# A state-space stage rewritten: convolutions on TensorE, the scan in two halves of the tokens with its input in PSUM

## The chip, the cores and the metric

One core of a Trainium2 chip runs the whole program. The metric is the device time of one execution in microseconds, the median of three runs. The engines are TensorE (PE; its weight loads are PEld), VectorE (DVE), ScalarE (ACT), GpSimd (POOL) and SyncE (SP, which here only issues transfers).

## The reference, cut to what matters

The program is a small transformer of eight sublayers on x of shape (1, 2048, 128), each followed by a residual add and a layer norm. The change touches the fifth sublayer, a selective state-space layer:

```python
def _L2_attn_ref(x, W_in, conv_x_w, conv_x_b, conv_z_w, conv_z_b, W_xdbl, W_dt, inv_dt, D, W_out, b_out):
    xz = x @ W_in
    xs, z = jnp.split(xz, 2, axis=-1)
    A = -jnp.tile(jnp.arange(1, D_STATE + 1, dtype=jnp.float32), (D_HALF, 1))
    xs = jax.nn.silu(_dw_conv(xs, conv_x_w, conv_x_b))   # 4 taps along the tokens, per channel
    z = jax.nn.silu(_dw_conv(z, conv_z_w, conv_z_b))
    x_dbl = xs @ W_xdbl
    dt_low, Bc, Cc = jnp.split(x_dbl, [DT_RANK, DT_RANK + D_STATE], axis=-1)
    dt = dt_low @ W_dt + inv_dt
    delta = jax.nn.softplus(dt + inv_dt)
    y = _selective_scan(xs, delta, A, Bc, Cc, D)
    y = jnp.concatenate([y, z], axis=-1)
    return y @ W_out + b_out
# _selective_scan, for each of 16 states n and each of 128 channels, over 2048 tokens:
#   h = exp(delta * A[n]) * h + (delta * u) * B[n];  y += h * C[n];  at the end y += u * D
```

## The kernel before

Everything stays in SBUF in float32. Activations lie as 128 channels (partitions) by 2048 tokens; PSUM has eight banks of 512 columns, so work goes in blocks of 512 tokens, numbered 0 to 3. Each stage is a class with one method for each engine (`pe`, `act`, `dve`, `pool`) that writes the engine's instructions in a fixed order by hand; engines meet only at counters (`wait_ge`, `then_inc`) and at a barrier (`Barrier.meet`, L128) where a stage begins. The state-space stage is `Mamba` (L1284).

**Entry.** PE turns x into its transpose XT before the barrier. Then it projects blocks of xs (L1348) and z (L1358); ACT copies them to SBUF with a margin of zeros (L1462, L1470). DVE does the convolution of xs as four shifted multiply-adds for each block (`taps`, L1594 and L1597), ACT applies silu to give U (L1468). PE multiplies U by W_xdbl (L1365, 64 rows for delta; L1368, 32 rows for B and C). B and C are split into three bfloat16 parts by turns between ACT and DVE (L1479 to L1488, L1544, L1549) and stored in SPL. PE makes dt (L1379), ACT its absolute value, exponential and logarithm (L1492, L1494, L1498), DVE the rest of the softplus and delta*u, called DU (L1554, L1559, L1561), for all 2048 tokens before the scan begins.

**Loop over the 16 states.** A selecting matmul of bfloat16 spreads row n of B over the 128 partitions, a block at a time (`rows_b`, L1441, PSUM banks 0 and 1). DVE multiplies that by DU into the SBUF tile H (`scale_in`, L1604). ACT makes the decay DA = exp(-(n+1)*delta) for 2048 tokens (L1517). DVE runs one scan over 2048 tokens (L1571) in place:

```python
            e.tensor_tensor_scan(h, da, h, 0.0, ALU.mult, ALU.add).then_inc(self.scan.sem)
```

`rows_c` (L1450, banks 2 and 3) spreads row n of C, ACT copies it to SBUF (`copy_c`, L1524, four buffers CS), POOL multiplies H by it in place (L1618), and PE adds the 16 products up in banks 4 to 7 with float32 matmuls by the identity (`add_up`, L1454). H has three buffers, DA two. The four taps of the convolution of z run on DVE over all 2048 tokens after states 1, 5, 9 and 13 (L1594, L1597).

**Tail.** ACT applies silu to z (L1508), DVE adds u*D (L1583), PE multiplies by W_out (L1416, L1417), DVE and ACT do the layer norm (L300 to L335).

## Time and profile before

| | |
|---|---|
| median of 3 runs | 2852.85 us (2852.33 to 2854.08) |
| the profiled execution | 2858.49 us, its span 2856.7 us |
| busy share of the span | PE 87%, DVE 73%, ACT 50%, POOL 43% |
| mean granted TensorE clock | 0.937 of full speed |
| the state-space stage, from its barrier to the next one | 685.3 to 905.3 us of the span |

A row names a line of the kernel, an engine, an operation and its tiles (out<-in). A float32 matmul instruction leaves two records on PE. Busy time of a stretch is the time in which the engine had at least one instruction under way; "idle before" says what released it. PEclk is the granted clock: 1.00 is 2.4 GHz, 0.50 is 1.2 GHz. WK is the large work area of SBUF (H, DA, CS, U, DE and others lie in it), W a weight area in which DU lies, PS is PSUM, CBB the selecting matrices, CB constants, NR small statistics.

### The profile page before, as it was taken

What the parts mean: (1) busy time and instruction counts of PE and PEld (TensorE: products, weight loads), DVE (VectorE), ACT (ScalarE), POOL (GpSimd) and SP (SyncE); (2) the same over time, 40 slices, a digit from 0 to 9 for tenths busy, and PEclk for the clock granted to TensorE, in tenths of its full rate; (3) what the DMA queues carried; (4) which work ended last, traced back from release to release, by engine and by line L of the source; (5) the groups of instructions that cost most, each with busy time, mean ns of one, the idle gap of its engine ahead of it and who ended that gap; (6) DMA issues with size and microseconds to landing.
All of it is one profiled execution on the core that took longest, in us unless ns stands there. A gap on an engine that the chain in (4) does not pass through costs nothing.

```text
span 2856.7 us, 39926 instructions
## 1 busy us (share of the span) xinstructions
PE 2472.2 (87%) x14878; PEld 1129.4 (40%) x14878; DVE 2076.3 (73%) x3166; ACT 1441.2 (50%) x2500; POOL 1227.9 (43%) x725
## 2 busy tenths in 40 slices
PE   6679996697576897789678999999999999999897
PEld 4333332444223565466433333333333333333344
DVE  7676666624887996599667888788887888788542
ACT  5455553343543775377433555445554555455462
POOL 1145552210596553355302555445554555455530
PEclk9699997798787999999899999999999999999999
DMA  5000001001000000000010000000000000000000
GB/s 200 1 1 1 1 1 45 1 1 41 0 0 15 1 1 1 1 1 1 16 41 1 9 9 9 9 9 8 9 9 8 9 9 9 5 9 9 9 1 15
DMA packets 20685, 37.38 MB, mean 13 GB/s; under 512 B 10446, under 2 KB 12622, under 8 KB 19468
## 3 DMA queue, kind: packets, MB, share of 16 engines
q1 hardware_dynamic: 20492, 34.83, 3.5%
q8 instruction: 118, 1.93, 0.3%
q14 instruction: 75, 0.61, 0.1%
HBM read 32.47 MB, written 2.35 MB: 12 GB/s over the span
## 4 chain that ended last, share of the span: by engine, by line
PE 54%; DVE 30%; issue 7%; POOL 4%; ACT 4%; DMA 0%; ACTq 0%; DVEq 0%; POOLq 0%; SPq 0%
PE PS L2429 12%; PE PS L2420 11%; PE PS L1173 6%; DVE NR L2636 5%; PE PS L2390 4%; POOL WK L1618 4%; DVE W L2654 2%; DVE WK L810 2%; DVE NR L265 2%; DVE WK L1968 2%; PE PS L1155 2%; DVE WK L1944 1%; PE PS L673 1%; PE PS L675 1%; PE PS L2376 1%
## 5 line engine op out<-in xcount | busy, mean ns | idle before, releaser
L2636 DVE TENSOR_REDUCE NR<-PS 128x2 f32<-128x1024 f32 x512 | 626.1, 1223 | 208.5 <-PE PS L2391 208.4
L2531 ACT ACTIVATE WK<-PS 128x1024 f32<-128x1024 f32 x512 | 496.7, 1021 | 489.6 <-PE PS L2420 415.8
L2706 POOL TENSOR_TENSOR W<-W,WK 128x1024 f32<-128x1024 f32 x224 | 527.1, 2353 | 481.7 <-DVE W L2654 413.0
L2429 PE MATMUL PS<-WK,W 128*64 128x512 f32 x2048 | 494.1, 603 | 0.0
L2420 PE MATMUL PS<-WK 64*128 64x512 f16 (+1 forms) x4096 | 484.9, 377 | 0.0
L2654 DVE TENSOR_TENSOR W<-W,WK 128x1024 f32<-128x1024 f32 x224 | 285.2, 1273 | 14.6 <-ACT WK L2531 14.2
L2420 PEld LDWEIGHTS PS<-WK 64*128 64x128 f16 (+1 forms) x4096 | 199.1, 94 | 219.7 <-ACT WK L2531 7.3
L870 POOL TENSOR_TENSOR WK<-WK 128x512 f32<-128x512 f32 x128 | 165.6, 1294 | 180.9 <-ACT WK L763 180.9
L2390 PE MATMUL PS<-WK 64*128 64x512 f16 x512 | 196.5, 384 | 37.5 <-DVE NR L2636 35.4
L2429 PEld LDWEIGHTS PS<-WK,W 128*64 128x64 f32 x2048 | 124.0, 136 | 249.6 <-issue 174.0
L2391 PE MATMUL PS<-WK 64*128 64x512 f16 x512 | 196.4, 384 | 0.0
L804 DVE TENSOR_TENSOR WK<-WK 128x512 f16<-128x512 f32 x128 | 103.9, 811 | 95.3 <-ACT WK L769 95.3
L1173 PE MATMUL PS<-WK,W 128*128 128x512 f16 x768 | 166.1, 379 | 0.0
L1618 POOL TENSOR_TENSOR WK<-WK 128x512 f32<-128x512 f32 x64 | 135.4, 2152 | 61.0 <-DVE WK L1571 61.0
L2390 PEld LDWEIGHTS PS<-WK 64*128 64x128 f16 x512 | 47.8, 93 | 286.5 <-DVE NR L2636 228.3
L1991 POOL TENSOR_TENSOR WK<-WK 128x512 f32<-128x512 f32 x64 | 113.4, 1793 | 93.9 <-DVE WK L1928 93.8
L1881 ACT ACTIVATE WK<-PS,WK 128x192 f32<-128x192 f32 (+1 forms) x256 | 103.7, 428 | 90.7 <-DVE WK L1968 90.7
L1999 POOL TENSOR_TENSOR WK<-WK 128x768 f32<-128x768 f32 (+1 forms) x64 | 91.5, 1449 | 102.8 <-DVE WK L1921 102.8
L769 ACT ACTIVATE WK<-WK 128x512 f16<-128x512 f32 x128 | 80.5, 629 | 97.6 <-DVE WK L810 97.0
L673 PE MATMUL PS<-WK 128*128 128x512 f16 x256 | 102.4, 400 | 25.9 <-DVE WK L793 25.2
L1173 PEld LDWEIGHTS PS<-WK,W 128*128 128x128 f16 x768 | 75.1, 98 | 90.6
L763 ACT ACTIVATE WK<-PS,CB 128x512 f32<-128x512 f32 x128 | 86.4, 675 | 36.9 <-PE PS L675 36.9
(368 smaller groups left out, 4404.3 us busy)
## 6 DMA issues: line engine op xcount, KB each, us to landing
XB<-l_rdens SPq DMA_DIRECT2D x62, 128.0 KB, 2.9
W<-in_mw SPq DMA_DIRECT2D x8, 512.0 KB, 12.3
W<-in_l2w SPq DMA_DIRECT2D x1, 3114.0 KB, 10.2
W<-in_f1w SPq DMA_DIRECT2D x1, 2816.0 KB, 18.8
W<-in_l3w SPq DMA_DIRECT2D x1, 2816.0 KB, 9.7
W<-in_f3w SPq DMA_DIRECT2D x1, 2816.0 KB, 10.1
W<-in_mw SPq DMA_DIRECT2D x8, 256.0 KB, 12.4
CBB<-in_cbb SPq DMA_DIRECT2D x1, 1360.0 KB, 8.4
```

The source lines that it names most:

```text
L673: e.matmul(k.bank(bk), self.WH[x][:, o:o + 128], self.XH[:, s_], start=True, stop=False)
L870: e.tensor_tensor(s1, s1, self.GS[i // 4 % 2], ALU.mult).then_inc(self.gated.sem)
L1173: i = e.matmul(k.bank(2 + (n + 2) % 6), wp[p][:, kb, o], src[q][:, kb, s_], start=kb == 0 and j == 0, stop=kb == 3 and j == 2)
L1618: e.tensor_tensor(h, h, self.CS[i % 4], ALU.mult).then_inc(self.hc.sem)
L2390: e.matmul(k.bank(6), q[0:64, ts_], self.KH[0:64, g, ks], start=True, stop=True)
L2391: e.matmul(k.bank(7), q[64:128, ts_], self.KH[64:128, g, ks], start=True, stop=True).then_inc(self.maxs.sem)
L2420: m = e.matmul(k.bank(2 * (kt % 2) + i), keys[own, :], queries[own, :], start=j == 0, stop=j == 3)
L2429: m = e.matmul(k.PS[64 * i:64 * i + 64, 4, :], self.V[:, kt, g, :], self.PTB[kt // 2 % 2][:, kt % 2, i, :], start=kt == 0, stop=kt == NT - 1)
L2531: e.activation(self.PTB[kt // 2 % 2][:, kt % 2, :, :], self.k.PS[:, 2 * (kt % 2):2 * (kt % 2) + 2, :], ACT.Exp, scale=1.0 / 64).then_inc(s ...
L2636: e.tensor_reduce(self.PM[ji % 2][:, u // 4, :, u % 4], self.k.PS[:, 6:8, :], AX.X, ALU.max).then_inc(self.maxes.sem)
L2654: e.tensor_tensor(ac, ac, p, ALU.add).then_inc(self.acc0.sem)
L2706: e.tensor_tensor(ac, ac, p, ALU.add).then_inc(self.acc1.sem)
```

## The change

- **Convolutions on PE.** The four taps of each convolution are folded into W_in: the tap weights arrive by one broadcast transfer (`sp_taps`), POOL multiplies them with W_in into eight 128x128 matrices (`taps`), before the barrier of the stage. A block of a convolution is then four accumulating float32 matmuls over XT shifted by one token each (`tap`). The separate projections, their copies by ACT and all taps on DVE are gone.
- **Two halves of the tokens.** The loop runs over 32 units u: states 0 to 15 for tokens 0 to 1023, then the same states for tokens 1024 to 2047. POOL keeps the last column of each scan of the first half in `state`, which is the start value in the second. Scans, DA and H are 1024 wide. Only blocks 0 and 1 are prepared before the loop; the B/C split, dt, the softplus and DU of blocks 2 and 3 are spread over units 1 to 14 on PE, ACT, DVE and POOL.
- **Scan inputs in PSUM.** `scale_in` writes to PSUM banks 2 and 3, and the scan reads them there, DA from SBUF, and writes H in SBUF. There is one pair of these banks, so `scale_in` of a unit waits for the scan of the unit before.
- **Banks.** 0 and 1 for rows of B, 2 and 3 for scan inputs, 4 and 5 for the sums of the current half, 6 alone for rows of C, 7 for blocks 2 and 3's preparation and, in units 10 to 25, for the gate z: one tap matmul for each unit (`pe_gate`), and a copy by ACT after every fourth (`act_gate`).
- **Small parts.** W_xdbl is one matmul of 96 rows for each block instead of two; the selecting matmuls use 96 partitions instead of 128. In the tail the output product of the first half stands ahead of the last two `add_up`. On SP the taps' transfer, which waits for the barrier ahead of the f1 stage, stands ahead of the transfer of the next layers' weights (L164).

The diff, cut to its core (the parts on `Loads`, the engines' lists and the loop's helpers; `add_up`, `copy_c`, `pe_conv`, `pe_low`, `pe_dt`, `pe_out` and the `act_` and `dve_` helpers do for one block or unit what the lines named above did):

```diff
@@ Loads, Mamba.__init__
+    def sp_taps(self, e, after_l1):
+        e.wait_ge(*after_l1.end(4))
+        e.dma_start(self.k.W2[:, 0:1024], self.k.A["cw"].broadcast_to([P, 1024])).then_inc(self.cw.sem, 16)
+        self.taps = [k.W2[:, i * 512:(i + 1) * 512].rearrange("p (j f) -> p j f", j=4) for i in range(2)]
+        self.CS = [wk(2048 + i * 512, 512) for i in range(4)]
+        self.DA = [wk(11264 + i * 1024, 1024) for i in range(2)]
+        self.H = [wk(13312 + i * 1024, 1024) for i in range(3)]
+        self.inv2, self.state = k.NR[:, 2, 100:101], k.NR[:, 2, 104:120]
-        RB = [wk(11270 + i * 2048, 2048) for i in range(5)]
-        self.DA, self.H = RB[0:2], RB[2:5]
@@ TensorE
+    def tap(self, e, side, b, n, bank):
+        k = self.k
+        j = ((1, 0, 2, 3) if not b else (1, 2, 3, 0))[n]
+        lo, hi = max(b * 512 + j - 1, 0), min((b + 1) * 512 + j - 1, T)
+        o = lo - (b * 512 + j - 1)
+        return e.matmul(k.PS[:, bank, o:o + hi - lo], self.taps[side][:, j, :], k.XT[:, lo:hi], start=n == 0, stop=n == 3)
+    def pe(self, e):
+        self.xt.ready(e, 3)
+        e.wait_ge(*self.folded(2))
+        self.pe_conv(e, 0)
+        self.pe_conv(e, 1)
+        self.pe_low(e, 0)
+        self.pe_low(e, 1)
+        self.pe_dt(e, 0)
+        self.pe_dt(e, 1)
+        self.pe_conv(e, 2)
+        self.pe_conv(e, 3)
+        self.rows_b(e, 0, 0)
+        self.rows_b(e, 0, 1)
+        for u in range(self.UNITS):
+            if u + 1 < self.UNITS:
+                self.rows_b(e, u + 1, 0)
+                self.rows_b(e, u + 1, 1)
+            self.rows_c(e, u, 0)
+            self.rows_c(e, u, 1)
+            if u:
+                self.add_up(e, u - 1, 0)
+                self.add_up(e, u - 1, 1)
+            if u == 1:
+                self.pe_low(e, 2)
+            elif u == 3:
+                self.pe_low(e, 3)
+            elif u == 5:
+                self.pe_dt(e, 2)
+            elif u == 7:
+                self.pe_dt(e, 3)
+            elif self.Z0 <= u < self.Z0 + 16:
+                self.pe_gate(e, u - self.Z0)
+        e.wait_ge(*self.zs(1))
+        self.pe_out(e, 0)
+        self.pe_out(e, 1)
+        self.add_up(e, 31, 0)
+        self.add_up(e, 31, 1)
+        self.pe_out(e, 2)
+        self.pe_out(e, 3)
+    def pe_gate(self, e, m):
+        b, n = m // 4, m % 4
+        if not n:
+            if not b:
+                e.wait_ge(*self.dpos(4))
+            else:
+                e.wait_ge(*self.zraw(b))
+        i = self.tap(e, 1, b, n, 7)
+        if n == 3:
+            i.then_inc(self.zconv.sem)
...
+    def rows_b(self, e, u, b):
+        i, n, t = 2 * u + b, u % 16, u // 16 * 2 + b
+        if u == 0:
+            e.wait_ge(*self.u(b + 1))
+        else:
+            e.wait_ge(*self.inp(i - 1))
+        if not u % 16:
+            e.wait_ge(*self.least(t + 1))
+        e.matmul(self.k.bank(i % 2), self.k.cb("selB", n * 128, (n + 1) * 128, p1=96), self.SPL[0:96, t * 512:(t + 1) * 512], start=True, stop=True).then_inc(self.selB.sem)
+    def rows_c(self, e, u, b):
+        i, n, t = 2 * u + b, u % 16, u // 16 * 2 + b
+        if i:
+            e.wait_ge(*self.cs(i))
+        else:
+            e.wait_ge(*self.u(3))
+        e.matmul(self.k.bank(6), self.k.cb("selC", n * 128, (n + 1) * 128, p1=96), self.SPL[0:96, t * 512:(t + 1) * 512], start=True, stop=True).then_inc(self.selC.sem)
...
@@ ScalarE
+    def act(self, e):
+        self.act_u(e, 0)
+        self.act_u(e, 1)
+        self.act_low(e, 0)
+        self.act_low(e, 1)
+        e.wait_ge(*self.twice(1))
+        self.act_abs(e, 0)
+        self.act_abs(e, 1)
+        self.act_exp(e, 0)
+        self.act_ln(e, 0)
+        self.act_ln(e, 1)
+        self.decay_of(e, 0)
+        self.decay_of(e, 1)
+        self.act_u(e, 2)
+        self.act_u(e, 3)
+        for u in range(self.UNITS):
+            self.copy_c(e, u, 0)
+            self.copy_c(e, u, 1)
+            if u == 2:
+                self.act_low(e, 2)
+            elif u == 4:
+                self.act_low(e, 3)
+            elif u == 5:
+                self.act_mid(e, 2)
+            elif u == 6:
+                self.act_abs(e, 2)
+                self.act_pos(e, 2)
+            elif u == 7:
+                self.act_mid(e, 3)
+            elif u == 8:
+                self.act_abs(e, 3)
+                self.act_pos(e, 3)
+            elif u == 9:
+                self.act_exp(e, 1)
+            elif u == 10:
+                self.act_ln(e, 2)
+                self.act_ln(e, 3)
+            elif u >= self.Z0 + 4 and (u - self.Z0) % 4 == 0 and u <= self.Z0 + 16:
+                self.act_gate(e, (u - self.Z0) // 4 - 1)
+            if u + 2 < self.UNITS:
+                self.decay_of(e, u + 2)
+        e.wait_ge(*self.zraw(4))
+        e.activation(self.ZS, self.ZS, ACT.Silu, bias=c("czb")).then_inc(self.zs.sem)
+        for b in range(NB):
+            self.ln.act(e, b)
+    def decay_of(self, e, u):
+        h, n = u // 16, u % 16
+        if not n:
+            e.wait_ge(*self.de(2 * h + 2))
+        if u >= 2:
+            e.wait_ge(*self.scan(u - 1))
+        e.activation(self.DA[u % 2], self.DE[:, h * 1024:(h + 1) * 1024], ACT.Exp, scale=-float(n + 1)).then_inc(self.decay.sem)
@@ VectorE
+    def dve(self, e):
+        e.tensor_scalar(self.inv2, c("invdt"), 2.0, None, ALU.mult).then_inc(self.twice.sem)
+        self.dve_rem(e, 0)
+        self.dve_mid(e, 0)
+        self.dve_rem(e, 1)
+        self.dve_mid(e, 1)
+        self.dve_least(e, 0)
+        self.dve_least(e, 1)
+        e.wait_ge(*self.twice(1))
+        for b in range(2):
+            e.wait_ge(*self.dabs(b + 1))
+            e.tensor_scalar(self.DE[:, b * 512:(b + 1) * 512], k.bank(self.TBANK[b]), self.inv2, 0.0, ALU.add, ALU.max).then_inc(self.dpos.sem)
+        for b in range(2):
+            self.delta(e, b)
+        for b in range(2):
+            self.delta_u(e, b)
+        for u in range(self.UNITS):
+            self.scale_in(e, u, 0)
+            self.scale_in(e, u, 1)
+            self.dve_scan(e, u)
+            if u == 3:
+                self.dve_rem(e, 2)
+            elif u == 5:
+                self.dve_rem(e, 3)
+            elif u == 16:
+                self.dve_y(e, 0)
+                self.dve_y(e, 1)
+        e.wait_ge(*self.biased(1))
+        for b in range(NB):
+            if b == 2:
+                self.dve_y(e, 2)
+                self.dve_y(e, 3)
+            e.wait_ge(*self.out(b + 1))
+            self.ln.dve(e, b, four(PS[:, b, :]))
+    def scale_in(self, e, u, b):
+        i, t = 2 * u + b, u // 16 * 2 + b
+        if not u % 16:
+            e.wait_ge(*self.du(t + 1))
+        if not u:
+            e.wait_ge(*self.high(2))
+            e.wait_ge(*self.rem(2))
+        else:
+            e.wait_ge(*self.scan(u))
+        e.wait_ge(*self.selB(i + 1))
+        e.tensor_tensor(self.k.bank(2 + b), self.DU[:, t * 512:(t + 1) * 512], self.k.bank(i % 2), ALU.mult).then_inc(self.inp.sem)
+    def dve_scan(self, e, u):
+        n = u % 16
+        if u >= 3:
+            e.wait_ge(*self.total(2 * (u - 3) + 2))
+        if u >= 16:
+            e.wait_ge(*self.kept(n + 1))
+        e.wait_ge(*self.decay(u + 1))
+        e.wait_ge(*self.inp(2 * u + 2))
+        first = self.state[:, n:n + 1] if u >= 16 else 0.0
+        e.tensor_tensor_scan(self.H[u % 3], self.DA[u % 2], self.k.PS[:, 2:4, :].rearrange("p a n -> p (a n)"), first, ALU.mult, ALU.add).then_inc(self.scan.sem)
@@ GpSimd
+    def pool(self, e):
+        k = self.k
+        e.wait_ge(*self.ld.cw(16))
+        for i in range(2):
+            w = self.w_in[:, i * 128:(i + 1) * 128].unsqueeze(1).broadcast_to([P, 4, 128])
+            e.tensor_tensor(self.taps[i], self.taps[i], w, ALU.mult).then_inc(self.folded.sem)
+        self.begin.meet(e)
+        e.tensor_tensor(k.X[:, :, :], k.X[:, :, :], k.c("bout").unsqueeze(1).broadcast_to([P, NT, P]), ALU.add).then_inc(self.biased.sem)
+        for u in range(self.UNITS):
+            h = self.H[u % 3]
+            e.wait_ge(*self.scan(u + 1))
+            if u in (8, 10):
+                e.wait_ge(*self.least(u // 2 - 1))
+            if u < 16:
+                e.tensor_copy(self.state[:, u:u + 1], h[:, 1023:1024]).then_inc(self.kept.sem)
+            for b in range(2):
+                i, s_ = 2 * u + b, slice(b * 512, (b + 1) * 512)
+                if b and u < 16:
+                    e.wait_ge(*self.kept(u + 1))
+                e.wait_ge(*self.cs(i + 1))
+                e.tensor_tensor(h[:, s_], h[:, s_], self.CS[i % 4], ALU.mult).then_inc(self.hc.sem)
+            if u in (7, 9):
+                e.wait_ge(*self.hc(2 * u + 2))
+                self.dve_least(e, 2 + (u - 7) // 2)
+            elif u in (11, 12):
+                self.delta(e, u - 9)
+            elif u in (13, 14):
+                self.delta_u(e, u - 11)
```

Where the orders differ, the new line numbers are: `tap` L1362, `rows_b` L1454, `rows_c` L1462, `add_up` L1472, U L1541, the decay L1582, `copy_c` L1589, the split of B and C on DVE L1638, `scale_in` L1672, the scan L1683.

PE, inside the loop, before (two thirds of a state: L1441 rows of B, L1450 rows of C, L1454 adding up):

```order
L1441 MATMUL PS<-WK,CBB 128x512 x2
L1450 MATMUL PS<-WK,CBB 128x512 x2
L1441 MATMUL PS<-WK,CBB 128x512 x2
L1454 MATMUL PS<-WK,CB 128x512 x2
L1450 MATMUL PS<-WK,CBB 128x512 x2
L1454 MATMUL PS<-WK,CB 128x512 x2
```

and now, in units that carry a tap of the gate (two units shown):

```order
L1454 MATMUL PS<-WK,CBB 128x512 x2
L1462 MATMUL PS<-WK,CBB 128x512 x2
L1472 MATMUL PS<-WK,CB 128x512 x2
L1362 MATMUL PS<-XT,W 128x512
L1454 MATMUL PS<-WK,CBB 128x512 x2
L1462 MATMUL PS<-WK,CBB 128x512 x2
L1472 MATMUL PS<-WK,CB 128x512 x2
L1362 MATMUL PS<-XT,W 128x512
```

Two units do the rows and the adding up of one state before; the float32 tap is new work in this loop.

DVE, the first states of the loop, before (L1604 scale, L1571 scan, which this list calls SCALAR_TENSOR_TENSOR, L1594 the first tap of z):

```order
L1604 TENSOR_TENSOR WK<-W,PS 128x512 x4
L1571 SCALAR_TENSOR_TENSOR WK<-WK 128x2048
L1604 TENSOR_TENSOR WK<-W,PS 128x512 x4
L1571 SCALAR_TENSOR_TENSOR WK<-WK 128x2048
L1604 TENSOR_TENSOR WK<-W,PS 128x512 x2
L1594 TENSOR_SCALAR WK<-WK,CB 128x2048
L1604 TENSOR_TENSOR WK<-W,PS 128x512 x2
```

and now, the first units (L1638 is a step of the B/C split of block 2):

```order
L1672 TENSOR_TENSOR PS<-W,PS 128x512 x2
L1683 SCALAR_TENSOR_TENSOR WK<-WK,PS 128x1024
L1672 TENSOR_TENSOR PS<-W,PS 128x512 x2
L1683 SCALAR_TENSOR_TENSOR WK<-WK,PS 128x1024
L1638 TENSOR_TENSOR WK<-PS,WK 32x512
L1672 TENSOR_TENSOR PS<-W,PS 128x512 x2
L1683 SCALAR_TENSOR_TENSOR WK<-WK,PS 128x1024
```

The scan has one input in SBUF and one in PSUM where it had two in SBUF, and the taps are gone.

PE, the entry, now (L1423 is U by W_xdbl, L1432 dt); before, the list went through L1348, L1358, L1365, L1368 and L1379 for all four blocks:

```order
L1362 MATMUL PS<-XT,W 128x512
L1362 MATMUL PS<-XT,W 128x511
L1362 MATMUL PS<-XT,W 128x512 x6
L1423 MATMUL PS<-WK,W 96x512 x2
L1432 MATMUL PS<-WK,W 128x512 x2
L1362 MATMUL PS<-XT,W 128x512 x5
```

The convolutions of blocks 2 and 3 stand behind dt of blocks 0 and 1 and ahead of the first rows of B.

## Rows read from the trace of the kernel before

**Rows 1.** Busy time by stretch of the stage: transposes, entry, loop, tail, end.

```profile
core 0: us, PE busy (x) PEld busy (x) DVE busy (x) ACT busy (x) POOL busy (x), PEclk, DMA share, GB/s
678.50:685.30 6.80, 3.88 (x16) 2.96 (x16) 4.40 (x16) 4.27 (x10) 0.00 (x0) 0.50 0.00 0
685.30:735.10 49.80, 30.80 (x47) 8.35 (x48) 28.54 (x46) 33.09 (x47) 6.31 (x2) 0.67 0.15 58
735.10:883.00 147.90, 104.26 (x243) 37.78 (x241) 129.24 (x80) 64.41 (x80) 130.42 (x60) 0.86 0.00 0
883.00:899.97 16.97, 11.88 (x72) 8.41 (x72) 10.16 (x42) 2.22 (x2) 4.94 (x4) 1.00 0.00 0
```

**Rows 2.** The chain of work, 735 to 905 us, shares by line.

```profile
by line: POOL WK L1618 62.0%; issue 12.9%; DVE WK L1571 8.8%; PE PS L1454 3.8%; DVE ST L307 2.1%; ACTq L129 1.6%; DVE WK L1604 1.5%; DVE X L300 1.4%; PE PS L1441 1.0%; DVE MV L310 0.9%; POOLq L129 0.8%; PE PS L1416 0.7%; ACT WK L1524 0.6%; 
```

**Rows 3.** Single lines: count, duration min/median/max in ns, first and last start.

```profile
L1571 DVE TENSOR_TENSOR_SCAN WK<-WK x16: 4424/5182/5551, 735.1 to 877.8; 128x2048 f32<-128x2048 f32 x16
L1618 POOL TENSOR_TENSOR WK<-WK x64: 1255/1268/5422, 739.6 to 886.8; 128x512 f32<-128x512 f32 x64
```

**Rows 4.** Timeline of DVE in the loop: start, length, engine, line.

```profile
748.69 2.28 DVE L1594 TENSOR_SCALAR WK<-WK,CB 128x2048 f32<-128x2048 f32 x1
750.89 1.27 DVE L1604 TENSOR_TENSOR WK<-W,PS 128x512 f32<-128x512 f32 x2
752.26 5.34 DVE L1571 TENSOR_TENSOR_SCAN WK<-WK 128x2048 f32<-128x2048 f32 x1
```

**Rows 5.** Timeline of PE and ACT in the loop at full clock.

```profile
808.12 1.16 ACT L1524 ACTIVATE WK<-PS 128x512 f32<-128x512 f32 x2 [1.30 <-PE PS L1450]
...
809.20 1.88 PE L1454 MATMUL PS<-WK,CB 128*128 128x512 f32 x4
...
810.92 0.59 PE L1450 MATMUL PS<-WK,CBB 128*128 128x512 bf16 x2
...
811.35 0.59 PE L1454 MATMUL PS<-WK,CB 128*128 128x512 f32 x1
811.39 0.60 ACT L1524 ACTIVATE WK<-PS 128x512 f32<-128x512 f32 x1 [0.32 <-PE PS L1450]
```

**Rows 6.** Granted clock of stretches of the loop and of two other stages.

```profile
743.30:750.10 6.80, 4.35 (x12) 1.54 (x11) 6.80 (x4) 2.65 (x3) 6.80 (x4) 1.00 0.00 0
750.10:753.60 3.50, 3.01 (x7) 0.99 (x6) 3.40 (x4) 2.07 (x3) 3.50 (x3) 0.51 0.00 0
...
384.90:446.40 61.50, 58.88 (x264) 24.43 (x262) 39.58 (x58) 38.11 (x64) 36.88 (x29) 1.00 0.00 1
962.00:1130.00 168.00, 148.90 (x1412) 108.16 (x1410) 141.35 (x254) 119.12 (x346) 79.67 (x51) 1.00 0.01 1
```

**Rows 7.** Groups of the entry, 685.3 to 735.1 us: busy, mean ns.

```profile
L1559 DVE TENSOR_TENSOR WK<-WK 128x512 f32<-128x512 f32 x4 | 2.7, 686 | 4.6 <-ACT WK L1498 4.6
L1604 DVE TENSOR_TENSOR WK<-W,PS 128x512 f32<-128x512 f32 x4 | 2.6, 684 | 0.1
L1492 ACT ACTIVATE WK<-PS,NR 128x512 f32<-128x512 f32 x4 | 2.5, 685 | 0.6 <-PE PS L1379 0.6
L1476 ACT ACTIVATE WK<-PS 64x512 f32<-64x512 f32 x4 | 2.3, 581 | 0.0
L1468 ACT ACTIVATE WK<-WK,CB 128x512 f32<-128x512 f32 x4 | 2.9, 722 | 6.2 <-DVE WK L1597 6.2
L1609 POOL MEMSET WK<- 32x2048 bf16 x1 | 1.8, 1799 | 105.4 <-ACTq L129 105.4
```

**Rows 8.** Timeline of ACT ahead of the first scan.

```profile
721.52 1.28 ACT L1494 ACT_TABLE_LOAD   x1
722.82 1.91 ACT L1494 ACTIVATE WK<-WK 128x2048 f32<-128x2048 f32 x1
```

**Rows 9.** Timeline of the tail.

```profile
889.25 2.73 DVE L1583 SCALAR_TENSOR_TENSOR WK<-WK,CB,PS 128x512 f32<-128x512 f32 x4 [6.24 <-PE PS L1454]
892.23 0.69 DVE L300 TENSOR_TENSOR X<-PS,X 128x512 f32<-128x512 f32 x1 [0.26 <-PE PS L1417]
...
894.16 0.66 DVE L300 TENSOR_TENSOR X<-PS,X 128x512 f32<-128x512 f32 x1
```

392 lines of the change are left out of this document (132 added, 260 removed).

## The prediction

> **What bounds the kernel now.** I read the stage by stretches first [rows 1]: entry 49.8 us, loop 147.9 us, tail 17.0 us; nothing outside the stage changes but two small things named below. In the loop POOL is busy 130.4 of 147.9 us and DVE 129.2; both look full, PE and ACT do not. The chain of waits [rows 2] puts 62% of its time on POOL's multiplication (L1618) and 9% on the scan. The single lines say why [rows 3]: POOL's multiplication takes 1.27 us, but up to 5.42; the scan takes 4.42 us at best, 5.18 as a rule. The long multiplication is one that fell beside a scan, the long scan one that had to let a multiplication finish: 4.42 + 4 x 1.25 = 9.4 us a state, against (877.8 - 735.1) / 15 = 9.5 measured [rows 3]. So the two take turns. The Trainium skill says it of the port ("SBUF — State Buffer", Who interferes with whom): a DVE instruction with two SBUF inputs and a GpSimd instruction that reads SBUF exclude each other. By that rule the trace agrees (5.42 against 1.27).
>
> DVE's `scale_in` (one SBUF, one PSUM input) holds 1.27 us a pair beside POOL [rows 4], so an instruction with one input in SBUF does not take turns. The new scan has that form.
>
> **Entry, step by step, from the barrier.** Conv 0 is eight PE passes. A pass is 0.43 us at full clock (four in 809.20 to 810.92) [rows 5]; the clock stands at half ahead of the barrier [rows 1], so I take four at 0.86 and four at 0.43: 5.1. Conv 1 follows to 8.6. U 0 and U 1 (0.72 each [rows 7]) hide behind it, U 1 ends at 9.5. The two products by W_xdbl end at 10.5, ACT's four copies (0.58) at 11.9, dt at 12.5, two absolute values (0.69) at 13.4. Then a table load 1.28, an exponential of 1024 columns (1.1, from 1.91 for 2048 and a fixed part), a load, two logarithms (0.7), a load: 19.7, and the decay to 20.8 [rows 7, 8]. DVE adds and multiplies twice each (0.69) after the logarithms, to 20.5, then scales (1.27), so the first scan starts at **22.0**. PE's convs of blocks 2 and 3 (16 x 0.43 = 6.9, from 12.5) end at 19.4, just under that cover; at half clock they would end at 26.3 and cost 4 to 5. Before it was 49.8 [rows 1]: **-27.8**. What goes is the taps on DVE, the preparation of blocks 2 and 3 and half of every exponential.
>
> **Loop.** DVE for a unit: from L1604 (0.684 for 512 columns at one step each) and the scan (4.424 for 2048 at two steps) [rows 3, 7] a column step is 1.04 ns and the fixed part 0.15, so a scan of 1024 takes 2.29. With the pair of scalings 1.27 and two gaps of 0.1 (750.89 + 1.27 to 752.26 [rows 4]) this is 3.76. No row shows DVE writing PSUM. The nearest, L1604 that reads it and L1559 that doesn't, are alike (0.684 and 0.686) [rows 7], so I take the same; a gain I see no reason for, the upper end is a doubling of the scaling, 1.27 more a unit. The Trainium skill ("VectorE: DVE Perf Modes", The TRN2 errata) gives VectorE a fixed cost of 120 cycles with a PSUM source against 58: an estimate of 0.065 us more a scan, 2 us over 32; the rows on L1604 and L1559 don't bear it out, and the sum goes without it.
>
> POOL for a unit: two multiplications without turns, 2.5, a one-column copy in the first half, which I put at 0.2: under 3.76. Its six extra steps (1.3 at most each) in units 7 to 14 fit, since H has three buffers.
>
> PE for a unit: a bfloat16 matmul is 0.215 (two in 810.92 to 811.35), a float32 one 0.86, and ACT's copy starts 0.47 after its matmul and takes 0.60 [rows 5]. Rows of C now have one bank: the second matmul waits for the first copy, 0.47 + 0.60 + 0.1 = 1.17 where 0.215 would do. So 0.43 + 1.17 + 0.215 + 1.72 = **3.54**, just under DVE's 3.76; with a tap of the gate **4.40**, over it. In units 10 to 25 PE becomes the bound. Nothing is late behind the wait but the adding up, which has slack.
>
> - Units 0 to 9: 10 x 3.76 = 37.6. Four extra float32 matmuls (3.4) against a slack of 0.22 a unit: +1.2. ACT's silu of U 2 and U 3 with a load on either side (4.0) in unit 0 makes rows of C late: +1.5. Two B/C steps on DVE (0.68): +1.4. About 42.
> - Units 10 to 25: 16 x 4.40 = 70.4. The logarithms in unit 10 with two loads (4.0 on ACT, against 1.4 of slack a unit): +1.5. u*D on DVE at unit 16, mostly slack: +0.5. About 72.5.
> - Units 26 to 31 to the end of the last scan: 5 x 3.76 + 2.29 = 21.
> - Clock: it fell behind stretches in which PE stood idle for much of the time, waiting for POOL (busy 4.35 of 6.80 us, then half clock [rows 6]), and stayed full in stages where PE was busy 89% and 96% of the time. The new loop has no such wait, and pure passes fill some 74% of it; I put 5% of it at half clock, +2.5.
>
> Sum 138 against 147.9: **-9.8**. The gain here is small because the port's turn-taking (9.5 a state) is replaced by PE's 8.8 in half of the loop, by DVE's 7.5 in the rest.
>
> **Tail.** From the last scan: silu of z ends at 2.1 (it starts when the last copy of C is done), the product of blocks 0 and 1 and their sums and statistics (1.93 each, 892.23 to 894.16 [rows 9]) run to 8.2, in the shade of POOL's last multiplication and the last two addings up, u*D of blocks 2 and 3 to 9.6, their products to 11.1, statistics to 14.9. Before, the wait for POOL and PE (883.0 to 889.25) came first: 17.0. **-2.0**.
>
> **At nothing.** POOL's folding (two of 1.3) lies in the 105 us in which POOL does nothing ahead of the barrier [rows 7]; uncovered it is 2.6. The taps' transfer (512 KB) is issued earlier still, at the barrier ahead of f1, and the one on SP that it delays (L164) is only used in the stage after this one. Rows of B with 96 partitions stream the same 512 columns: no gain.
>
> **Sum.** 27.8 + 9.8 + 2.0 = 39.6. On the profiled execution: 2858.49 - 39.6 = 2818.9. It ran 5.6 above the median, which I subtract: 2852.85 - 39.6 = **2813**.
>
> **Rivals.**
>
> 1. PE has more room than I think: the gate's taps and the wait for rows of C hide. Then DVE bounds throughout, 31 x 3.76 + 2.3 + 1.5 = 120.4, loop -27.5: **2795**. For it: the 0.1 for PE's restart is a guess, and PE may catch up in the units without a tap. Against it: the order is fixed, and rows of C have one bank.
> 2. The scan still takes turns with POOL, or PSUM as a target is slow. Turns: 2.29 + 2.5 + 0.2 = 5.0 a unit, loop 157, **2832**. Doubled scaling gives 31 x 5.03 + 2.3 = 158, the same. For it: no row shows a scan that reads PSUM or an output to it. Against: L1604 has the same mix of inputs and doesn't take turns [rows 4].
> 3. The clock falls, and the kernel becomes slower. Pure passes in the loop are 32 x 2.58 + 20 x 0.86 = 100 us at full clock. With a share s at half clock they take 100 / (1 - s/2). Before, the loop ran at 0.86, so s = 0.28 [rows 1]: 116 instead of 102, about **2827**. All of it at half clock: 6.0 a unit and 7.7 with a tap, loop 215, **2890**. It turns slower from s of about 0.6, where the passes have grown by 40 us. For it: short bursts; against: PE was emptier before, and still had 0.86. The Trainium skill ("TensorE: Matmul & The Clock Gate", Part 1) says that the clock is halved after idleness and restored after sustained work; by that rule the more even load keeps it, and the trace agrees, half-clock stretches following waits [rows 6].
> 4. It doesn't do what it says: the first half's preparation isn't shortened since ACT's chain (three table loads) rules. That chain is in my sum; if every step of the entry were as long as before, it would be -11.8 only, **2841**.
>
> **How the numbers follow.** The forecast (2805 to 2824) gets 0.53, rival 1 and mixtures of it 0.19, rival 2 and the milder clock of rival 3 0.17, the entry's failure 0.03, about the same time 0.03, slower 0.05. The range 2795 to 2835 holds the first three but for their tails, some 0.85. A measurement of this kernel can tell about 0.2%, 5.7 us: faster 0.92, same 0.03, slower 0.05.
>
> **What would show it.** Right: the first scan some 22 us after the barrier; scans of 2.3 us at even intervals of 3.8, then 4.4 in the units with a tap; POOL's multiplications near 1.27 throughout; DVE's idle time in units 10 to 25 released by PE's rows of B. Wrong: multiplications of 2 us or more beside scans; scans over 2.6; a scaling over 0.8; a granted clock below 0.9 in the loop; DVE never waiting for PE.

## The result and the profile after

The changed kernel takes 2816.99 us (median of four runs, 2814.71 to 2824.1) against 2853.47 us for the one before on the same chip (2852.33 to 2858.71): a ratio of 0.9874, 95% interval 0.9862 to 0.9887, or 36.5 us less. The forecast was 2813, that is 39.6 us less than the 2852.85 it started from. The profiled execution took 2824.1 us, its span is 2822.0.

First the stage by the same stretches as [rows 1]: transposes, entry, loop, tail.

```profile
core 0: us, PE busy (x) PEld busy (x) DVE busy (x) ACT busy (x) POOL busy (x), PEclk, DMA share, GB/s
677.80:684.70 6.90, 3.88 (x16) 2.98 (x16) 4.50 (x17) 4.26 (x10) 0.05 (x1) 0.50 0.00 0
684.70:706.46 21.76, 20.56 (x44) 8.05 (x44) 8.67 (x16) 14.52 (x17) 4.45 (x1) 0.92 0.35 134
706.46:846.19 139.73, 107.95 (x287) 41.45 (x288) 117.05 (x98) 82.86 (x118) 87.30 (x84) 0.95 0.00 0
846.19:863.00 16.81, 10.63 (x71) 8.09 (x70) 9.18 (x40) 3.52 (x3) 2.49 (x2) 1.00 0.00 0
```

The entry went from 49.8 to 21.8 us, the loop from 147.9 to 139.7, the tail from 16.9 to 16.4 (the stretch is taken to 863.0; the last statistics end at 862.6). In the loop POOL fell from 130.4 to 87.3 busy, DVE from 129.2 to 117.1, and PE is at 108. No engine is full, so the waits have to say what holds the rest. In the chain of waits of the changed kernel, 706 to 863 us:

```profile
by line: PE PS L1472 29.3%; ACT WK L1589 13.8%; PE PS L1462 12.3%; PE PS L1362 7.6%; issue 6.8%; PE PS L1454 6.5%; ACT WK L1582 4.0%; DVE ST L312 2.2%; DVE X L305 1.6%; ACT L1582 1.6%; PE PS L1484 1.5%; PE PS L1423 1.4%; PE PS L1432 1.3%; P
```

POOL's 62% [rows 2] is gone. Its place is taken by the adding up (L1472), rows of C (L1462), the copy between them (L1589) and the gate's taps (L1362). The scan (L1683) isn't among the lines shown. The single lines, which answer to [rows 3] and [rows 4] (count, shortest/median/longest in ns):

```profile
L1683 DVE TENSOR_TENSOR_SCAN WK<-WK,PS x16: 2286/2287/2289, 706.5 to 775.1; 128x1024 f32<-128x1024 f32 x16
...
L1683 DVE TENSOR_TENSOR_SCAN WK<-WK,NR,PS x16: 2346/2347/2348, 779.5 to 843.8; 128x1024 f32<-128x1024 f32 x16
...
L1672 DVE TENSOR_TENSOR PS<-W,PS x64: 689/690/697, 705.1 to 843.0; 128x512 f32<-128x512 f32 x64
...
L1712 POOL TENSOR_TENSOR WK<-WK x64: 1261/1270/1284, 709.8 to 847.5; 128x512 f32<-128x512 f32 x64
```

The longest of 64 multiplications on POOL is 1.284 us, where it was 5.422, and the 16 scans of a half differ by 2 to 3 ns among themselves. Nothing takes turns any more. A scaling that writes PSUM takes 0.690, where it was 0.684 into SBUF. The second half's scans carry the state in as a pointer (NR) and take 2.347, 0.06 more than the first half's.

From the timeline of PE, ACT and DVE in a unit with a tap of the gate, 797.68 to 802.05:

```profile
797.68 0.39 PE L1462 MATMUL PS<-WK,CBB 96*128 96x512 bf16 x1 [0.75 <-ACT WK L1589]
...
797.91 1.88 PE L1472 MATMUL PS<-WK,CB 128*128 128x512 f32 x4
...
799.63 1.02 PE L1362 MATMUL PS<-XT,W 128*128 128x512 f32 x2
...
800.49 0.60 PE L1454 MATMUL PS<-WK,CBB 96*128 96x512 bf16 x2
...
800.92 0.38 PE L1462 MATMUL PS<-WK,CBB 96*128 96x512 bf16 x1
801.40 0.60 ACT L1589 ACTIVATE WK<-PS 128x512 f32<-128x512 f32 x1 [1.69 <-PE PS L1462]
...
802.05 0.39 PE L1462 MATMUL PS<-WK,CBB 96*128 96x512 bf16 x1 [0.75 <-ACT WK L1589]
```

This is the wait for the one bank of rows of C: from 801.13, when the first matmul has streamed, PE waits until ACT's copy ends at 802.00. The unit takes 802.05 - 797.68 = 4.37 us. VectorE waits for PE in such units, here for the rows of B of another one:

```profile
773.64 1.30 DVE L1672 TENSOR_TENSOR PS<-W,PS 128x512 f32<-128x512 f32 x2 [0.65 <-PE PS L1454]
```

How evenly the scans come shows where this counts. These are the distances between the starts of neighbouring scans, in us:

```
units  0 to  9: 3.72 3.72 7.16 4.46 3.83 4.46 4.13 3.75 4.64 3.75                                  43.6
units 10 to 25: 3.75 5.86 6.65 4.37 4.37 4.40 8.21 3.81 3.81 3.81 3.81 3.86 4.37 4.37 4.36 4.36   74.2
units 26 to 30: 4.37 3.81 3.81 3.81 3.81, and the last scan 2.35                                   22.0
```

Three places stand out: unit 2 (7.16), units 11 and 12 (5.86 and 6.65), unit 16 (8.21). Unit 2 first, from the timeline of PE and DVE:

```profile
714.37 3.62 PE L1472 MATMUL PS<-WK,CB 128*128 128x512 f32 x4
...
719.63 1.29 DVE L1672 TENSOR_TENSOR PS<-W,PS 128x512 f32<-128x512 f32 x2 [3.45 <-PE PS L1454]
```

And the stretch by itself, columns as above, in which PEclk stands third from the end:

```profile
708.50:718.80 10.30, 7.34 (x12) 2.56 (x13) 7.41 (x7) 6.10 (x8) 5.55 (x7) 0.50 0.00 0
```

From 706.5 to 713.4 ACT does silu of U 2 and U 3 with a table load on either side, two copies and a decay. Rows of C come late for it, and PE works through what has piled up at half clock: four passes of adding up in 3.62 us, where they take 1.88 at full clock. The next rows of B stand behind them in PE's order, and DVE waits 3.45 us for those. Units 11 and 12 go the same way; ACT, DVE and PE there:

```profile
754.60 1.28 ACT L1574 ACT_TABLE_LOAD   x1
755.89 1.33 ACT L1574 ACTIVATE WK<-WK,CB 128x512 f32<-128x512 f32 x2
...
757.24 1.28 ACT L1582 ACT_TABLE_LOAD   x1
758.54 1.06 ACT L1582 ACTIVATE WK<-WK 128x1024 f32<-128x1024 f32 x1
...
759.68 2.29 DVE L1683 TENSOR_TENSOR_SCAN WK<-WK,PS 128x1024 f32<-128x1024 f32 x1 [1.88 <-ACT WK L1582]
...
760.13 0.61 PE L1462 MATMUL PS<-WK,CBB 96*128 96x512 bf16 x1 [3.30 <-ACT WK L1589]
...
764.91 1.29 DVE L1672 TENSOR_TENSOR PS<-W,PS 128x512 f32<-128x512 f32 x2 [2.94 <-PE PS L1454]
```

The scan of unit 12 waits for its decay, which stands behind the second table load; ACT's copy of a row of C stands behind that decay, PE waits 3.30 us for it and catches up in part at half clock (granted 0.68 from 760 to 765), and DVE waits 2.94 us for the rows of B behind. Unit 16, DVE alone:

```profile
784.73 1.60 DVE L1688 SCALAR_TENSOR_TENSOR WK<-WK,CB,PS 128x512 f32<-128x512 f32 x2 [2.92 <-PE PS L1472]
...
786.25 1.29 DVE L1672 TENSOR_TENSOR PS<-W,PS 128x512 f32<-128x512 f32 x2
...
787.67 2.35 DVE L1683 TENSOR_TENSOR_SCAN WK<-WK,NR,PS 128x1024 f32<-128x1024 f32 x1
```

DVE's u*D (L1688) waits 2.92 us for the last adding up of the first half, which PE does only behind rows of C of the unit after it; the scaling of the next unit stands behind u*D on DVE.

The tail answers to [rows 9]:

```profile
846.44 1.28 ACT L1535 ACT_TABLE_LOAD   x1
847.74 2.00 ACT L1535 ACTIVATE WK<-WK,CB 128x2048 f32<-128x2048 f32 x1
...
851.97 0.69 DVE L305 TENSOR_TENSOR X<-PS,X 128x512 f32<-128x512 f32 x1 [5.79 <-PE PS L1485]
```

The product by W_out starts at 849.84, when silu of all 2048 columns has ended.

For the experiments I use three numbers of each trace: when the first scan starts, how long the loop lasts (to the end of the last scan) and the tail (from there to the last statistics of the norm). Two executions of the same kernel differ by 3.7 us in the first number (706.5 here, 702.8 in the repeat below). Of these 1.8 lie in the entry, whose first 3.4 us had half clock here and full clock in the repeat; the other 1.9 lie ahead of the barrier. Loop and tail agree within 0.2. So small differences are read from the loop, not from the total. The tail needs more care: it had full clock in both executions of the changed kernel, but a mean granted 0.90 in e1, e3, e4 and e6 and 0.81 in e5, where a part of the products by W_out ran at half clock. With one profile of each, whether the edit or chance decides that is not shown. Each ratio is to the kernel before as measured beside it (medians 2853.47, 2855.57 for e1 to e4, 2854.13 for the repeat and e5 to e7, 2854.95 for e8 and f1).

| kernel | median (runs) | ratio to before, 95% | first scan | loop | tail |
|---|---|---|---|---|---|
| before | 2853.47 | | 735.1 | 147.9 | 16.9 |
| changed | 2816.99 (4) | 0.9874, 0.9862 to 0.9887 | 706.5 | 139.7 | 16.4 |
| changed, repeated | 2815.09 (4) | 0.9856, 0.984 to 0.9871 | 702.8 | 139.9 | 16.4 |
| e1_scan_from_sbuf | 2837.01 (5) | 0.9931, 0.9918 to 0.9945 | 702.4 | 158.8 | 16.7 |
| e2_one_gate_tap | 2809.41 (5) | 0.9841, 0.9828 to 0.9854 | 701.4 | 133.4 | 15.4 |
| e3_interleave | 2805.95 (5) | 0.9827, 0.9814 to 0.984 | 701.7 | 127.4 | 17.2 |
| e4_skip_late | 2816.11 (4) | 0.9858, 0.9843 to 0.9873 | 707.1 | 138.6 | 17.9 |
| e5_both | 2810.37 (5) | 0.9837, 0.9823 to 0.985 | 706.9 | 126.5 | 18.3 |
| e6_logs_aside | 2803.05 (5) | 0.9825, 0.9811 to 0.9838 | 701.9 | 125.3 | 17.4 |
| e7_silu_split | 2796.59 (5) | 0.9798, 0.9784 to 0.9811 | 702.4 | 125.3 | 14.5 |
| e8_best_from_sbuf | 2826.26 (5) | 0.9897, 0.9882 to 0.9912 | 702.5 | 152.0 | 14.8 |
| f1_before_one_tap | 2848.55 (8) | 0.9979, 0.9968 to 0.9989 | 729.0 | 141.5 | 19.1 |

### The profile page after: what moved, and what is told of

The parts are those of the page before. It is cut to its first block, busy times and chain, and to the rows that moved or that the text cites. A ratio compares the mean times of both kernels' runs of the same rounds, so it can differ in the third digit from the quotient of the medians.

```text
span 2822.0 us, 40142 instructions
## 1 busy us (share of the span) xinstructions
PE 2465.9 (87%) x14918; PEld 1133.0 (40%) x14918; DVE 2043.2 (72%) x3152; ACT 1442.9 (51%) x2509; POOL 1183.1 (42%) x748
## 3 DMA queue, kind: packets, MB, share of 16 engines
HBM read 32.99 MB, written 2.35 MB: 13 GB/s over the span
## 4 chain that ended last, share of the span: by engine, by line
PE 57%; DVE 29%; issue 7%; ACT 5%; POOL 1%; DMA 0%; ACTq 0%; DVEq 0%; SPq 0%; POOLq 0%
PE PS L2530 12%; PE PS L2521 12%; PE PS L1178 6%; DVE NR L2737 5%; PE PS L2491 5%; DVE W L2755 2%; DVE WK L815 2%; DVE NR L270 2%; DVE WK L2069 2%; PE PS L1160 2%; PE PS L1472 2%; DVE WK L2045 1%; DVE WK L267 1%; PE PS L2477 1%; PE PS L678 1%
## 5 line engine op out<-in xcount | busy, mean ns | idle before, releaser
L875 POOL TENSOR_TENSOR WK<-WK 128x512 f32<-128x512 f32 x128 | 165.6, 1294 | 180.3 <-ACT WK L768 180.3
L2092 POOL TENSOR_TENSOR WK<-WK 128x512 f32<-128x512 f32 x64 | 113.5, 1795 | 93.9 <-DVE WK L2029 93.7
L815 DVE SCALAR_TENSOR_TENSOR WK<-PS,WK 128x512 f32<-128x512 f32 x128 | 95.0, 742 | 11.0 <-PE PS L680 11.0
## 6 DMA issues: line engine op xcount, KB each, us to landing
W<-in_l3w SPq DMA_DIRECT2D x1, 2816.0 KB, 10.3
W<-in_mw SPq DMA_DIRECT2D x8, 256.0 KB, 12.3
```

The source lines that it names most:

```text
L815: e.scalar_tensor_tensor(out=self.HF[j % 3], in0=k.bank(2 + j % 3), scalar=self.MB1[:, x * 8 + 4 + kb:x * 8 + 5 + kb], in1=self.S1[j % 3], ...
L875: e.tensor_tensor(s1, s1, self.GS[i // 4 % 2], ALU.mult).then_inc(self.gated.sem)
```

## The experiments

### The scan's input back in SBUF

```diff
+        if u >= 3 and not b:
+            e.wait_ge(*self.total(2 * (u - 3) + 2))
...
-        e.tensor_tensor(self.k.bank(2 + b), self.DU[...], self.k.bank(i % 2), ALU.mult)...
+        e.tensor_tensor(self.H[u % 3][:, b * 512:(b + 1) * 512], self.DU[...], self.k.bank(i % 2), ALU.mult)...
...
-        e.tensor_tensor_scan(self.H[u % 3], self.DA[u % 2], self.k.PS[:, 2:4, :].rearrange("p a n -> p (a n)"), first, ...)
+        e.tensor_tensor_scan(self.H[u % 3], self.DA[u % 2], self.H[u % 3], first, ...)
```

> The changed kernel with one part undone: scale_in writes to H in SBUF, the scan reads both inputs there. Theory (the scan and GpSimd's multiplication take turns when both scan inputs are in SBUF): multiplications of 3 us or more beside scans again, scans of up to 3.5 us, a unit of about 2.29 + 2 x 1.25 + 0.2 = 5.0 us where it was 3.8 to 4.4, so +15 to +22 us over the changed kernel's 2817, about 2835. Rival (halves, convolutions on TensorE and the better spread work carry the gain, the place of the scan's input does not matter): multiplications stay at 1.27, the time stays within 3 us of 2817.

Measured: 2837.01, against 2816.99 and 2815.09 for the changed kernel; the loop 158.8, 19 us longer. Single lines of this kernel:

```profile
L1685 DVE TENSOR_TENSOR_SCAN WK<-WK x16: 2291/3008/3142, 702.4 to 774.4; 128x1024 f32<-128x1024 f32 x16
...
L1685 DVE TENSOR_TENSOR_SCAN WK<-WK,NR x16: 2351/3277/3286, 784.2 to 857.9; 128x1024 f32<-128x1024 f32 x16
...
L1714 POOL TENSOR_TENSOR WK<-WK x64: 1260/1272/3265, 705.8 to 862.5; 128x512 f32<-128x512 f32 x64
```

Three instructions of DVE's timeline:

```profile
824.80 3.28 DVE L1685 TENSOR_TENSOR_SCAN WK<-WK,NR 128x1024 f32<-128x1024 f32 x1
...
828.12 1.28 DVE L1674 TENSOR_TENSOR WK<-W,PS 128x512 f32<-128x512 f32 x2
...
829.54 3.28 DVE L1685 TENSOR_TENSOR_SCAN WK<-WK,NR 128x1024 f32<-128x1024 f32 x1
```

The turns are back with the one operand: the same scan takes 3.28 instead of 2.35, a multiplication up to 3.27, and a unit 829.54 - 824.80 = 4.74. All else is as in the changed kernel, but for a wait before a tile of H is written, and in these rows VectorE doesn't stand at it. So it is the place of the scan's input that ends the turns, and here it is worth some 20 us of the 36.5. The rule named in the prediction (the Trainium skill, "SBUF — State Buffer", Who interferes with whom) fits these rows: a VectorE instruction with two inputs in SBUF contends with GpSimd's reads, one with at most one doesn't. How a pointer for the start value counts the rule doesn't say; in the changed kernel it made no turns (at most 1.284 on POOL).

The 19 us aren't 31 equal parts. Against the changed kernel a unit takes 0.93 more where VectorE bounds and 0.36 more in the five units from 22 to 26, where PE bounded. Unit 15 alone takes 9.83 instead of 4.40:

```profile
773.86 4.47 POOL L1714 TENSOR_TENSOR WK<-WK 128x512 f32<-128x512 f32 x2
...
778.39 2.08 PE L1472 MATMUL PS<-WK,CB 128*128 128x512 f32 x2 [2.03 <-POOL WK L1714]
...
782.73 1.34 DVE L1674 TENSOR_TENSOR WK<-W,PS 128x512 f32<-128x512 f32 x2 [5.45 <-PE PS L1454]
```

POOL, slowed by the turns and with its steps for blocks 2 and 3 to do, had fallen behind; PE waited for its product and then worked at half clock, and VectorE waited for PE. A unit by itself came to 4.73, not to the 5.0 that was expected.

Without that operand the loop would have been longer than before (158.8 against 147.9, with the second half's preparation in it), and only the entry would have gained.

### One tap of the gate's convolution

Twelve of the 16 float32 products of the gate's convolution are left out in this kernel, so the gate is computed from one tap.

```diff
-        i = self.tap(e, 1, b, n, 7)
         if n == 3:
-            i.then_inc(self.zconv.sem)
+            e.matmul(self.k.bank(7), self.taps[1][:, 1, :], self.k.XT[...], start=True, stop=True).then_inc(self.zconv.sem)
```

> The changed kernel with 12 of the 16 gate taps left out (each block of the gate keeps one tap in place of four; this leaves out that part of the convolution of z). Theory (TensorE bounds units 10 to 25 by the tap it carries): the intervals of the scans there fall from 4.37 to 3.81 us in 12 units, -6 to -8 us. Rival (DVE or another engine would hold these units anyway, the taps fill idle time of TensorE): within 2 us of the changed kernel.

Measured: 2809.41; the loop 133.4, 6.3 less than the changed kernel's. Units 13 to 15 take 3.75 to 4.27, and from 17 on the scans come at 3.81 throughout; the 4.37 are gone. Units 2 and 11 are as before, units 12 and 16 are shorter (5.78 instead of 6.65, 6.62 instead of 8.21). So in the units with a tap PE did bound the loop, and what bounds without it is DVE. The 6.3 us lie in the range that was expected, but not where the theory put them: it had 12 units going from 4.37 to 3.81. Units 13 to 15 and 21 to 26 gave 3.8, and 2.5 came from the stalls at units 12 and 16, which PE's shorter work cut too. Units 17 to 20 gave nothing, though three of them lost a tap: they took 3.81 already, since PE had got ahead during the stall of unit 16. Twelve taps are 12 x 0.86 = 10.3 us on PE, so 4.0 of it had been hidden.

### Rows of C and the adding up in turn

```diff
             self.rows_c(e, u, 0)
-            self.rows_c(e, u, 1)
             if u:
                 self.add_up(e, u - 1, 0)
+            self.rows_c(e, u, 1)
+            if u:
                 self.add_up(e, u - 1, 1)
```

> The changed kernel with another order on TensorE alone: the first adding up of a unit stands between the two matmuls for rows of C, in the time in which the second waits for ScalarE's copy. Theory (TensorE's path for a unit is 3.5 or 4.4 us because it stands idle about 0.75 us at that wait): the wait is filled, a unit with a tap needs 3.6, the scans of units 10 to 25 come every 3.8 us, and the matmuls of blocks 2 and 3 in units 1 to 7 cost less: -8 to -12 us, about 2807. Rival (the copy chain through ScalarE bounds, not TensorE's occupation): no change, since the copies then come later.

Measured: 2805.95; the loop 127.4, 12.3 less. The timeline of a unit with a tap now:

```profile
785.00 0.38 PE L1463 MATMUL PS<-WK,CBB 96*128 96x512 bf16 x1
...
785.22 1.02 PE L1473 MATMUL PS<-WK,CB 128*128 128x512 f32 x2
...
786.13 0.39 PE L1463 MATMUL PS<-WK,CBB 96*128 96x512 bf16 x1
...
786.36 1.02 PE L1473 MATMUL PS<-WK,CB 128*128 128x512 f32 x2
...
787.22 1.02 PE L1362 MATMUL PS<-XT,W 128*128 128x512 f32 x2
```

And its chain of waits, 706 to 863 us, by line:

```profile
by line: DVE WK L1684 28.8%; issue 14.5%; DVE PS L1673 11.0%; PE PS L1473 8.5%; PE PS L1362 3.3%; PE PS L1463 3.0%; PE PS L1485 2.5%; PE PS L1486 2.2%; POOL WK L1713 2.1%; PE PS L1455 2.0%; PE PS L244 2.0%; ACT WK L1590 1.8%; ACTq L129 1.7%
```

ACT's copy (0.47 + 0.60) now lies beside the first half of the adding up, and PE stands still for 0.05 us (two passes of 0.43 from 785.22 on end at 786.08, the next matmul starts at 786.13) instead of 0.9. In the chain the scan (L1684) leads with 28.8% and the scaling follows; scans come at 3.81 in every unit from 17 on, taps or none. The same matmuls in another order gave more than leaving out twelve of them, since it shortens PE's work in all units, those at the stalls too: unit 2 shrinks from 7.16 to 4.60, unit 12 from 6.65 to 5.19 and unit 16 from 8.21 to 5.84. The rival (the chain of copies through ScalarE bounds) falls with it.

### The u*D of the first half one unit later

```diff
-            elif u == 16:
+            elif u == 17:
```

> The changed kernel with the addition of u*D for blocks 0 and 1 after the scan of unit 17 instead of 16. Theory (the interval of 8.2 us there is VectorE waiting 2.9 us for the last adding up of the first half, and 1.6 us of its own): the wait goes, the interval is at most 5.5, -2.5 to -4 us in all. Rival (the wait moves on to TensorE, whose adding up of unit 16 waits for it): within 1 us.

Measured: 2816.11, the same as the changed kernel (2816.99 and 2815.09); the loop 138.6, 1.2 less. Unit 16 now takes 4.34 instead of 8.21, but the units behind it take 4.98, 3.81, 4.31, 4.36, 4.37 where they took 3.81 (the last 3.86): what DVE no longer waits for it waits for later, because PE is the bound and no longer ahead. A stall of 4.4 us was worth 1.2 of the loop, and nothing that the total shows: the tail is 1.5 longer, with half clock on the products by W_out. The theory (2.5 to 4 us less) was wrong; the rival (within 1 us) is right of the total and nearly right of the loop.

### The changed kernel again, and both edits together

> The changed kernel itself once more, on the chip of the runs beside it. Every theory expects some 36 to 39 us under the kernel before, ratio 0.987.

Measured: 2815.09 (2808.83 to 2817.26), the loop 139.9, the tail 16.4: loop and tail repeat within 0.2. This is what small differences are held against.

The next kernel has the edits of e3 and e4.

> The order on TensorE (adding up between the two rows of C) and the later addition of u*D together. If each removes its own wait: the interval of 5.8 us after unit 16 goes to at most 5.4 and nothing new comes, -9 to -12 us against the changed kernel, 1 to 2 us under the new order alone. If VectorE merely waits elsewhere (the 1.4 us of u*D cannot be hidden where VectorE is the bound): the same as the new order alone, within 1 us.

Measured: 2810.37, 126.5 for the loop, 0.9 less than with the first alone. Unit 16 takes 3.81 instead of 5.84, unit 17 takes 4.98 instead of 3.81: VectorE's own work on u*D only moves there. Loop and tail together are 144.8 against 144.6, so this is the second of the two cases expected. The median is 4.4 above that of e3, of which the loop shows nothing: in the two profiles the first scan starts 5.3 later (706.9 against 701.7) and the tail is 1.1 longer, at a lower granted clock (0.81 against 0.90). The total can't rank these two, the loop can.

### The logarithms behind the decay, the gate two units later

On top of e5:

```diff
-    Z0 = 10
+    Z0 = 12
...
-            elif u == 10:
-                self.act_ln(e, 2)
-                self.act_ln(e, 3)
...
+            if u == 10:
+                self.act_ln(e, 2)
+                self.act_ln(e, 3)
```

> As the run with both, and the gate's taps in units 12 to 27, with the two logarithms of blocks 2 and 3 behind the decay of unit 12 instead of ahead of it. Theory (the two table loads and two logarithms, 4 us on ScalarE, hold back the decay and then the rows of C while TensorE has a tap to carry too): the intervals after units 10 to 15, 3.5 us over the plain 3.8 in all, shrink by 2 us or more. Rival (ScalarE is short of time there whatever the order): the excess only moves to later units, within 1 us.

Measured: 2803.05, the loop 125.3, 1.2 less than e5. Units 10 to 15 take 3.75, 3.75, 4.20, 5.20, 3.75 and 4.34 where e5 had 3.75, 4.65, 5.18, 4.27, 3.74 and 4.59; the two table loads are on ACT as before, and only a part of them hides. That is less than the 2 us of the theory and about the 1 us of the rival. The edit changes two things, the place of the logarithms and the units of the taps, and which of them gave the 1.2 wasn't measured.

### Silu of the gate in four blocks

On top of e6, with `pe_out` waiting for the block it needs:

```diff
-        e.activation(self.ZS, self.ZS, ACT.Silu, bias=c("czb")).then_inc(self.zs.sem)
+        for b in range(NB):
+            s_ = slice(b * 512, (b + 1) * 512)
+            e.activation(self.ZS[:, s_], self.ZS[:, s_], ACT.Silu, bias=c("czb")).then_inc(self.zs.sem)
```

> As the run before, and silu of the gate in four blocks instead of one instruction, so that the output product of block 0 waits for 0.7 us of it and not 2.0. Theory (the tail begins with the chain last copy of C, table load, silu, product): the tail from the last scan to the last statistics shrinks from 16.4 to about 15.1, -1 to -1.5 us. Rival (the products or VectorE's statistics bound the tail): no change.

Measured: 2796.59, the tail 14.5 against 17.4 (16.4 in the changed kernel). Its timeline:

```profile
827.34 1.28 ACT L1538 ACT_TABLE_LOAD   x1
...
828.64 2.56 ACT L1538 ACTIVATE WK<-WK,CB 128x512 f32<-128x512 f32 x4
829.46 0.46 PE L1485 MATMUL PS<-WO,WK 128*128 128x128 f32 x2 [1.82 <-issue]
...
831.59 0.69 DVE L305 TENSOR_TENSOR X<-PS,X 128x512 f32<-128x512 f32 x1 [3.90 <-PE PS L1486]
```

Silu takes 0.56 us longer in four pieces, but PE starts at 829.46, when the first is done, and DVE's first sum comes 3.90 us after the last scan instead of 5.79. The pieces by themselves are worth 1.3: PE starts 1.77 after the last scan, in e6 it was 3.05. In e6 a stretch of half clock lay on these products (the first two took 0.75 us where here 0.46), and the rest of the 2.9 between the two tails is the clock's. Against the changed kernel, where the clock was full in the tail, it is 1.9, of which 0.6 comes from the order of e3: the last copy of C, and with it the table load, is earlier (the load starts 0.35 ahead of the last scan's end, in the changed kernel 0.27 behind it). So the pieces gave what was expected, 1 to 1.5. The medians lie 6.5 apart, more than loop and tail explain. This is the fastest version: 57.5 us (2.0%) under the kernel before, 2854.13, and 18.5 under the changed kernel (2815.09); 16.5 of it stand in loop and tail.

### One tap of z in the kernel before

Three of the four taps of the gate's convolution are left out here, in the kernel before. On DVE they took 3.34, 2.40 and 3.34 us, 9.1 in all.

```diff
-        e.wait_ge(*self.zconv(4))
+        e.wait_ge(*self.zconv(1))
...
-            if n % 4 == 1:
-                if n == 1:
-                    e.wait_ge(*self.xz(8))
+            if n == 1:
+                e.wait_ge(*self.xz(8))
                 self.taps(e, self.ZS, self.PZ, 0, T, "czw", [n // 4], self.zconv, 0)
```

> The kernel before, with three of the four taps of the gate's convolution on VectorE left out (that part of the convolution of z is not computed). Three instructions of 2.3 to 3.3 us, 9.1 us together, stand in the loop behind states 5, 9 and 13. Theory (the scan and GpSimd's multiplication take turns, VectorE has time between): most of it lay in time in which VectorE would have waited for its turn, so the loop of 147.9 us loses 3 to 5 us. Rival (VectorE is simply full, 87% busy in the loop): it loses 8 to 9 us, and moving the taps to TensorE alone would have paid that much.

Measured: 2848.55 against 2854.95, a ratio of 0.9979 (0.9968 to 0.9989), so 3 to 9 us less. The loop is 6.4 shorter, which is between the theory (3 to 5) and the rival (8 to 9). The tail is 2.2 longer; DVE waits there for POOL's multiplications and the adding up:

```profile
878.92 2.72 DVE L1582 SCALAR_TENSOR_TENSOR WK<-WK,CB,PS 128x512 f32<-128x512 f32 x4 [8.41 <-PE PS L1454]
```

It was 6.24 [rows 9]. Of this 0.9 is POOL, which ends that much later behind the last scan; the rest goes with half clock on the adding up, in the first 6 us of a tail that had full clock before. So 9.1 us taken from DVE give 6.4 in the loop and 4.3 over loop and tail: not all of DVE's time bounds the kernel before, as long as the scan takes turns with POOL. How much of the tail's part belongs to the edit is not shown.

### The fastest version with the scan's input in SBUF

The last kernel has the edit of e1 on top of e7.

> The fastest version so far (order on TensorE, later u*D, logarithms aside, silu in blocks) with the scan's input in SBUF again. Theory (taking turns costs the same 4.73 us a unit whether TensorE is the bound or not, and in the changed kernel TensorE's 4.37 hid part of the price): intervals of 4.7 against 3.8 us, the loop some 150 us instead of 125, +22 to +28 us, more than the 16 to 20 us that the same undoing cost in the changed kernel. Rival (the price is the same as there): +16 to +20.

Measured: 2826.26, 29.7 above e7; the loop 152.0, 26.7 longer. From DVE's timeline:

```profile
824.87 2.99 DVE L1688 TENSOR_TENSOR_SCAN WK<-WK,NR 128x1024 f32<-128x1024 f32 x1
827.90 1.28 DVE L1677 TENSOR_TENSOR WK<-W,PS 128x512 f32<-128x512 f32 x2
829.32 2.99 DVE L1688 TENSOR_TENSOR_SCAN WK<-WK,NR 128x1024 f32<-128x1024 f32 x1
```

A unit takes 829.32 - 824.87 = 4.45 instead of 3.81. The same operand costs 19 us of loop in the changed kernel and 26.7 here, so a part of the price was hidden behind PE there, as the 0.36 against 0.93 a unit in e1 says too. The loop of 152 matches the expected 150 in part by luck: a unit costs 0.64 more and not 0.9, and 9.7 of the 26.7 us lie in two units, 12 and 15 (8.34 and 9.85 against 4.20 and 4.33), in which PE waits for POOL and VectorE for PE.

## Why the prediction was right, point by point

**Entry, -27.8 forecast, -28.0 measured.** First scan 21.8 us after the barrier, forecast 22.0. Inside it one step was wrong and fell into a shadow: silu's table load (1.28) comes only behind ACT's wait for the first convolution (it starts at 690.16), not ahead of it, but U 1 was ready at 694.25, 9.5 after the barrier as in the sum. The clock was half for the first 3.4 us. In the repeat it was full from ahead of the barrier on, and the entry took 20.0 (682.8 to 702.8).

**Loop, -9.8 forecast, -8.2 measured.** The sizes of one unit held: 3.75 forecast 3.76 in the first half, 4.37 forecast 4.40 with a tap. In the second half it is 3.81, because the scan with a pointer for its start value takes 2.347 where I had 2.29; that is at most 16 x 0.06 = 0.9 us of the loop, less where PE bounds. By parts:

| term | forecast | measured |
|---|---|---|
| units 0 to 9 | 42 | 43.6, the clock's share in it |
| of it B/C steps on DVE | 1.4 | 1.4 (units 3 and 5, 0.71 each) |
| of it four extra float32 matmuls | 1.2 | 1.3 (units 6 and 8, 0.38 and 0.89) |
| of it silu of U 2 and U 3 | 1.5 | 3.4 (unit 2), with the clock |
| units 10 to 25 | 72.5 | 74.2 |
| of it the logarithms | 1.5 | 3.8 over 4.37 (units 11 and 12) |
| of it u*D | 0.5 | 3.8, of which 2.7 given back in units 17 to 21 |
| units 26 to the end | 21 | 22.0, unit 26 still at 4.37 |
| clock | 2.5 | in units 0 to 2 and 12; mean granted 0.95, so 10% at half |

The terms that were mis-sized are the three stalls. "Silu makes rows of C late: +1.5" and "clock +2.5" are largely one event: 10 of the some 14 us at half clock (708.5 to 718.8) end in unit 2, where PE was catching up, and the share at half clock was twice the 5% put down. "The logarithms +1.5 (4.0 on ACT, against 1.4 of slack a unit)" counted slack over units, but the next decay and the copy of C stand right behind them in ACT's order, and PE behind the copy. "u*D mostly slack" missed that DVE's order sets it ahead of the next scaling while PE's order sets what it waits for behind rows of C: 4.4 us of stall. It came out near the forecast only because PE, the bound there, used the stall to get ahead; e4 shows it from the other side (the stall gone, 1.2 gained in the loop). So the sum for one unit was understood, while that the loop's total lies within 1.6 us of the forecast is partly luck: the stalls cost about twice what was put down for them, and units 17 to 21 gave 2.7 back.

**Tail, -2.0 forecast, -0.6 measured.** The step that failed is "silu of z ends at 2.1". With a load of 1.28 and silu's 2.00 that has the last copy of C end 1.2 ahead of the last scan's end. It ended at 846.43, 0.26 behind it, since PE, the bound up to unit 26, gave the rows of C late; silu ended at 3.6, and the first sum came at 5.8 where I had 4.3. In e2, with twelve taps fewer on PE, the load starts 0.70 ahead of the last scan's end (834.78), and the tail is 15.4 with silu whole:

```profile
834.08 1.28 ACT L1534 ACT_TABLE_LOAD   x1
```

In e7, with the order of e3 and silu in pieces, the first sum comes at 3.9 and the tail is 14.5.

**At nothing.** POOL's folding lies at 579 to 583 us, where POOL is idle, as forecast, though a step takes 1.71 and not 1.3:

```profile
L1697 POOL TENSOR_TENSOR W<-W x2: 1714/1714/1715, 579.2 to 580.9; 128x512 f32<-128x512 f32 x2
```

**The rivals.** Rival 1 (PE has room, DVE bounds throughout, 2795) was wrong of this kernel, by its 4.37 a unit, and right about the one that e3 makes of it: with the wait gone DVE bounds, 127.4 us, with the stalls, against the rival's 120.4. Rival 2 (turns stay, or PSUM is slow as a target) falls with the single lines; e1 made its turns come true. That the loop then took 158.8 where the rival had 157 is partly luck: a unit by itself took 4.73 and not 5.0, and unit 15 with its 9.83 and the stall at unit 16 (8.40) make up for it. The estimate from the Trainium skill beside the sum ("VectorE: DVE Perf Modes", The TRN2 errata: more fixed cost for a PSUM source, 0.065 us a scan) isn't borne out: the scan with a PSUM input takes 2.287, and the shortest in e1 with both inputs in SBUF takes 2.291. Rival 3 (clock) needed a share of 0.28 at half clock for its milder case and about 0.6 to be slower; measured is 0.10. Rival 4 (entry not shortened) falls with 21.8.

Not tried: the entry's parts, convolutions on PE and halves of the tokens, were not run one without the other, so how its 28 us divide between them rests on the working alone. The sum was 39.6; the medians give 36.5, and in the repeat 39.0 (2854.13 - 2815.09). Tail and loop fell short by 3.0 together; with the 36.5 this is nearly the whole difference, while the 39.0 of the repeat, whose loop and tail are the same, shows that the totals carry 2 to 3 us of the stages around.

## What to carry to other kernels

Where VectorE and GpSimd both run near full, look at the longest time of one instruction of a line, not at its mean: taking one input of the VectorE instruction from PSUM took away turns that cost some 20 us here, for 6 ns more an instruction that writes there. Its real price was two banks: rows of C had to share one, and another order on TensorE that hides this took 12.3 us off the loop. Where two matmuls share one PSUM bank with a copy between them, put independent matmuls between the two, and the copy hides. And ask of a stall whether its engine is the bound: 4.4 us of waiting on VectorE were worth 1.2 of the loop and nothing in the total, because TensorE got ahead meanwhile.

## What the runs showed that I had not expected

- A scan whose start value is a pointer takes 2.347 us instead of 2.287 for 1024 columns, and doesn't take turns with GpSimd's multiplication (at most 1.284) as long as one of the two large inputs is in PSUM.
- When the turns come, the scan's length is set by the rhythm of the two engines: 3.28 us in e1 at 4.73 a unit, 2.99 in e8 at 4.45, for the same instruction.
- The same kernel's stage began 2 us apart in two profiles and its first scan 3.7 apart; the 1.8 us of the entry go with its granted clock (0.92 against 1.00). That is more than the steps of e4, e5 or e6 gained in the loop.
- The tail had full clock in the changed kernel and in e2, e7 and e8, and stretches of half clock in e1 and e3 to e6, by which tails with the same work differ by 1 us and more (17.4 in e6 against 16.4). What decides it is open.
